# One fused layer on one Trainium2 core: the second gate, the residual and the last expert's factor moved

## What is computed

```python
xbc = silu(conv(xbc))                      # 4 taps along the tokens, 2560 channels
scores = einsum(C, B) * decay * dt         # inside chunks of 128 tokens
y = (scores @ X + (C * exp(cum)) @ Hprev + D_skip * X).reshape(B, L, D_INNER)
y = rmsnorm(y * silu(z), gnorm_w)          # "y * silu(z)" is the gate
x = x + layernorm(u + y @ out_proj_w.T)    # the residual
...
w = silu(einsum(h, down_embed[indices]) * softmax(top 8 of scores))
x = x + layernorm(silu(h @ W_up.T) @ W_down.T + einsum(w, up_embed[indices]))
```

## Time and profile before

| what | value |
|---|---|
| median of 3 runs (lowest to highest) | 2841.09 us (2840.73 to 2841.52) |
| the profiled execution, its own time | 2840.37 us |
| span of its trace, first to last instruction | 2838.7 us |
| mean granted TensorE clock | 0.972 |
| busy: PE, PEld, DVE, ACT, POOL | 95%, 78%, 86%, 61%, 74% |
| HBM read and written | 25.37 MB, 8.39 MB (12 GB/s) |

### The profile page before, as it was taken

The page is one execution under the profiler, slowest core; times in us unless marked ns, Lnnn a source line. Parts: engine busy times, 40 slices in busy tenths (PEclk is TensorE's granted clock), DMA queues, the critical chain, the costliest instruction groups (busy, mean ns, idle before and its releaser), DMA issues. The chain is left out here.

```text
span 2838.7 us, 50280 instructions
## 1 busy us (share of the span) xinstructions
PE 2684.0 (95%) x14720; PEld 2215.7 (78%) x14720; DVE 2449.3 (86%) x6310; ACT 1737.2 (61%) x3656; POOL 2100.9 (74%) x2689
## 2 busy tenths in 40 slices
PE   5899999999999999999999999999999999999985
PEld 4778887878887878887878887878887878887864
DVE  4588898998888998889898889988889988989985
ACT  4566666666666566666666666666666666666643
POOL 3377777877777877777877777877777877777866
PEclk9999999999999999999999999999999999999998
DMA  3000000000000000000000000000000000000000
GB/s 133 8 8 12 5 7 11 11 11 11 4 7 11 11 11 11 4 7 11 11 11 11 4 7 11 11 11 11 4 7 11 11 11 8 7 7 11 8 5 8
DMA packets 28182, 34.23 MB, mean 12 GB/s; under 512 B 2672, under 2 KB 27248, under 8 KB 27440
## 3 DMA queue, kind: packets, MB, share of 16 engines
q1 hardware_dynamic: 28144, 33.77, 3.8%
HBM read 25.37 MB, written 8.39 MB: 12 GB/s over the span
## 5 line engine op out<-in xcount | busy, mean ns | idle before, releaser
L1079 DVE SCALAR_TENSOR_TENSOR acc<-bank,cw,acc 128x253 f32<-128x253 f32 (+2 forms) x1920 | 773.5, 470 | 0.0
L1405 PE MATMUL bank<-hT,w_in 128*128 128x256 f32 x2560 | 606.3, 382 | 11.4 <-DVE acc L1079 10.8
L594 POOL TENSOR_TENSOR Em<-ee 128x1024 f32<-128x1024 f32 x256 | 578.8, 2280 | 11.3 <-issue 11.3
L1405 PEld LDWEIGHTS bank<-hT,w_in 128*128 128x128 f32 x2560 | 485.0, 192 | 118.2 <-issue 44.5
L1238 DVE SCALAR_TENSOR_TENSOR Em<-Em,p 128x1024 f32<-128x1024 f32 x256 | 407.1, 1590 | 0.0
L609 POOL TENSOR_TENSOR W<-W,Em 128x1024 f32<-128x1024 f32 x128 | 337.0, 2633 | 8.5 <-ACT Em L887 0.3
L755 ACT ACTIVATE acc<-bank,cb,cw 128x256 f32<-128x256 f32 x640 | 325.1, 561 | 0.0
L1247 DVE TENSOR_TENSOR Em<-Em,products 128x1024 f32<-128x1024 f32 x256 | 310.9, 1214 | 4.5
L887 ACT ACTIVATE Em<-Em,rden 128x1024 f32<-128x1024 f32 x256 | 292.0, 1142 | 33.9 <-DVE Em L1247 33.9
L1574 PE MATMUL products<-w_de,h2T 128*128 128x512 f32 x512 | 234.5, 601 | 17.7 <-DVE Em L1247 17.7
L736 ACT ACTIVATE xbcT<-acc 128x512 f32<-128x512 f32 x320 | 200.6, 627 | 74.1 <-DVE acc L1079 74.0
(11 more groups left out here) (196 smaller groups left out, 5578.9 us busy)
## 6 DMA issues: line engine op xcount, KB each, us to landing
x_in<-x_dram SPq DMA_DIRECT2D x32, 256.0 KB, 2.7
x_res<-x_dram SPq DMA_DIRECT2D x32, 256.0 KB, 2.7
out_dram<-f SPq DMA_DIRECT2D x32, 256.0 KB, 2.2
w_in<-in_wT_dram SPq DMA_DIRECT2D x1, 3080.0 KB, 12.0
w_up<-upT_dram SPq DMA_DIRECT2D x1, 1024.0 KB, 14.7
w_de<-down_eT_dram SPq DMA_DIRECT2D x1, 1024.0 KB, 16.7
w_down<-downT_dram SPq DMA_DIRECT2D x1, 1024.0 KB, 18.7
w_ue<-up_e_dram SPq DMA_DIRECT2D x1, 1024.0 KB, 20.8
```

Of the source, the lines that this page charges most:

```text
L594: nc.gpsimd.tensor_tensor(Em[:, k], bc(ee[:, k, 0:XD], 2, KEYS), bc(ee[:, k, XD:XD + KEYS], 1, XD), ALU.mult).then_inc(E_done.sem, 1)
L1079: ins = V.scalar_tensor_tensor(acc[:, r, a, ahead:], ps[:, a * TOK:(a + 1) * TOK - ahead], cw[:, t, k:k + 1], acc[:, r, a, ahead:], ALU.mu ...
L1405: last = mm(ring[j % 2][:, a * TOK:(a + 1) * TOK], w_in[:, k, at:at + P], hT[:, k, :], start=k == 0, stop=k == DK - 1)
```

## The change

- VectorE: `tail_residual(e)` comes ahead of convolution 0. `ffn_mask(e, 0, 2)` goes from before the second gate to behind the state step. `ffn_choose` multiplies all of `clz` by `rden` in one instruction (128x160); `ffn_last` is the copy of `last_a` alone.
- ScalarE: the silu of `clz` takes `last_a` as its scale; `ffn_norm(f)` goes behind the second square.
- GpSimd: the map of chunk 1, head 0 waits for the second gate. The order is then: root of y, map of head 1, `tail_root3(g)`, `tail_root4(g)` (before: in the next turn), first sum of `W`, maps of heads 2 and 3. The second decay of the state goes ahead of `ffn_root`.
- TensorE: no clearing matmul; the first product of `ffn_down` starts the bank.

```diff
 def weigh(e, c, *heads, gate=None):
+    if gate is not None:
+        pool.wait_ge(y_done.sem, y_done.at(gate, CH - 1))
...
 # GpSimd's do_group
-                if b:
-                    tail_root4(e)
...
                     mixer_scale(g, 1)
+                    mixer_decay(g, 1)
                 if c:
                     ffn_root(f)
-                if a:
-                    mixer_decay(g, 1)
-                if b:
-                    weigh(e, 1, 0, 1)
+                if b:
+                    weigh(e, 1, 0, gate=g)
                 if a:
                     mixer_root_y(g)
                 if b:
+                    weigh(e, 1, 1)
+                if a:
+                    tail_root3(g)
+                    tail_root4(g)
+                if b:
                     collect(e, 0, 1)
-                if a:
-                    tail_root3(g)
-                if b:
                     weigh(e, 1, 2, 3)
...
 # ScalarE, ffn_experts; ffn_norm(f) moves from behind mixer_yT(g, 0) to behind mixer_square(g, 1)
-                    nc.scalar.activation(cls[:], clz[:, c], ACT.Silu, accum_out=clsum[:, c:c + 1])\
+                    nc.scalar.activation(cls[:], clz[:, c], ACT.Silu, scale=last_a[:, 0:1],
+                                         accum_out=clsum[:, c:c + 1])\
...
 # VectorE
+                V.tensor_tensor(masked, masked, bc(rden[:].rearrange("p c h -> p (c h)"), 2, NC), ALU.mult)\
...
-                V.scalar_tensor_tensor(clz[:, c], clz[:, c], last_a[:, 0:1], bc(rden[:, c], 2, NC),
-                                       ALU.mult, ALU.mult).then_inc(clz_done.sem, 1)
...
-                conv(0)
                 if b:
                     tail_residual(e)
-                conv(1)
+                conv(0, 1)
...
                     ffn_times(e, 0, 1)
-                    ffn_mask(e, 0, 2)
                 if a:
                     mixer_gate(g, 1)
                     mixer_step(g, 1)
                 if b:
+                    ffn_mask(e, 0, 2)
                     ffn_times(e, 0, 2)
...
 # TensorE, ffn_down
-                    mm(f0[:], zero_b[:], mask_b[:].rearrange("p h t -> p (h t)"), start=True, stop=False)
...
-                              start=False, stop=False)
+                              start=c == 0 and i == 0, stop=False)
```

More of the change, by code:

```diff
@@ L123, in sandwich @@
         ident_b = sb("ident_b", [P, P], BF16)
-        zero_b = sb("zero_b", [P, P], BF16)
         mask_b = sb("mask_b", [P, 4, P], BF16)
@@ L270, in sandwich @@
         Z_done = sig("Z_done", CH * RH)
-        clz_done, cls_done = sig("clz_done", CH), sig("cls_done", CH)
+        clz_done, last_done, cls_done = sig("clz_done"), sig("last_done", CH), sig("cls_done", CH)
         W_part, W_done = sig("W_part", CH * (RH - 1)), sig("W_done", CH)
@@ L341, in _ @@
             nc.gpsimd.memset(mask_b[:], 0.0).then_inc(own_pool, own.one())
-            nc.gpsimd.memset(zero_b[:], 0.0).then_inc(own_pool, own.one())
             nc.gpsimd.memset(halo[:], 0.0).then_inc(own_pool, own.one())
@@ L582, in tail_root4, with weigh @@
                 nc.gpsimd.tensor_tensor(shift4[:], rs4[:], neg_mean4[:], ALU.mult).then_inc(root4.sem, 1)
-            def weigh(e, c, *heads):
+            def weigh(e, c, *heads, gate=None):
+                if gate is not None:
+                    pool.wait_ge(y_done.sem, y_done.at(gate, CH - 1))
                 for h in heads:
@@ L654, in do_group @@
                 if b:
-                    collect(e, 0, 1)
+                    weigh(e, 1, 1)
                 if a:
                     tail_root3(g)
+                    tail_root4(g)
                 if b:
+                    collect(e, 0, 1)
                     weigh(e, 1, 2, 3)
@@ L875, in ffn_experts @@
                 if 0 in heads:
-                    act.wait_ge(clz_done.sem, clz_done.at(e, c))
+                    act.wait_ge(clz_done.sem, clz_done.at(e))
+                    act.wait_ge(last_done.sem, last_done.at(e, c))
                     if c or later(e):
@@ L994, in do_group @@
                     mixer_yT(g, 0)
-                if c:
-                    ffn_norm(f)
                 if b:
@@ L1001, in do_group @@
                     mixer_square(g, 1)
+                if c:
+                    ffn_norm(f)
                 if b:
@@ L1221, in ffn_choose @@
                 V.reciprocal(rden[:].rearrange("p c h -> p (c h)"), den[:]).then_inc(rden_done.sem, 1)
+                dve.wait_ge(rden_done.sem, rden_done.at(e))
+                dve.wait_ge(own_dve, own.n)
+                V.tensor_tensor(masked, masked, bc(rden[:].rearrange("p c h -> p (c h)"), 2, NC), ALU.mult)\
+                    .then_inc(clz_done.sem, 1)
             def ffn_last(e, c):
                 dve.wait_ge(A_ps.sem, A_ps.at(e, c))
-                dve.wait_ge(rden_done.sem, rden_done.at(e))
-                V.tensor_copy(last_a[:], fA[:, EXPERTS - 1:]).then_inc(own_dve, own.one())
-                dve.wait_ge(own_dve, own.n)
-                V.scalar_tensor_tensor(clz[:, c], clz[:, c], last_a[:, 0:1], bc(rden[:, c], 2, NC),
-                                       ALU.mult, ALU.mult).then_inc(clz_done.sem, 1)
+                if c or later(e):
+                    dve.wait_ge(cls_done.sem, cls_done.at(e, c - 1))
+                V.tensor_copy(last_a[:], fA[:, EXPERTS - 1:]).then_inc(last_done.sem, 1)
             def ffn_mask(e, c, *heads):
```

## The result

The changed kernel takes 2936.55 us (median of 4 runs, 2934.81 to 2941.0) against 2841.31 us before: ratio 1.034, 95% interval 1.032 to 1.036, some 95 us slower. The forecast was 2903 us, slower, with a range up to 2958. The execution with the trace took 2941.0 us by itself, 4.5 above the median.

What follows compares the result with a forecast made beforehand. TensorE, busy 95%, was taken as the bound, waiting 2.13 us a turn for the second gate. A turn: +0.63 - 0.2 + 1.63 = +2.06 us; 30 turns give +62 on 2841.09, so 2903 us, range 2830 to 2958.

Steps and rivals of the forecast that it cites:

- The gate: TensorE's 2.13 us wait for the second gate, and the 1.63 us clock fall behind it, go each turn.
- What is late next: At mixer_pair 2, TensorE waits 4.4 us for convolution 0 and starts 0.63 us later than before.
- the one by the addition: On VectorE, GpSimd's map of head 1 asks 0.35 us earlier; the store's addition ends at 1373.75, not 1372.4.
- step 5: VectorE's mask and ffn_times of head 3 end at 1376.15; ffn_A also waits for this, about 0.2 us.
- 11.66: TensorE's microseconds at full clock from the transposes to pair 2, making it ready there at 1379.5.
- Step 7: VectorE's residual and convolution 0 take 4.51 us with GpSimd quiet, ending at 1383.9.
- The clock: TensorE's clock falls behind pair 2 as it fell behind the gate, costing 1.63 us more a turn.
- rival B: Stall moves to pair 2, clock stays low longer, losing 3.4 us: +3.85 a turn, 2956 us; chance 0.20.
- A: Stall moves to pair 2 with one clock fall of 1.63 us: 2903 us; chance 0.48.
- The clearing matmul: On TensorE, dropping this 0.38 us matmul saves between 0 and 0.38 us a turn; 0.2 taken.
- The factor: On VectorE, ffn_last loses a multiplication per chunk and ffn_choose gains one of 128x160; nothing taken.
- The rule weighed: By the skill's shared-port rule, ffn_root's power on GpSimd could delay the gate some 0.7 us; not counted.

Runs made afterwards that it cites:

- e7: Changed kernel with GpSimd's map of chunk 1, head 1 moved behind root 3 and root 4: 2874.9 us, ratio to before 1.012.
- e1: Changed kernel with convolution 0 ahead of the residual again on VectorE, all else as changed: 2918.1 us, ratio to before 1.027.
- e2: Changed kernel plus five unneeded matmuls on TensorE between ffn_A and pair 2, filling the wait: 2877.4 us, ratio to before 1.013.
- e3: Kernel before plus the residual part alone: residual ahead of convolution 0, root 4 right behind root 3: 2873.3 us, ratio 1.013.
- e6: Kernel before with two unneeded matmuls filling the gate's wait and without the clearing matmul: 2795.2 us, ratio 0.984.
- e11: Kernel before plus the last expert's factor part alone (one 128x160 multiplication, last_a as silu scale): 2843.0 us, ratio 1.001.
- e9: Changed kernel with convolution 0 first, ffn_best behind convolution 7, tail_sum and residual later, GpSimd's map explicitly waiting for ffn_times: 2762.8 us, ratio 0.973.

## Why the prediction was right, and where it was off

It laid the new order out on the old turn's times. The new trace, moved by 1414.72 - 1364.17 = 50.55 us so that the product `Yn` stands where it did, gives:

| step | forecast | measured |
|---|---|---|
| gate ends | 1367.5 | 1367.58 |
| mask of head 2 ends | 1370.55 | 1370.64 |
| store's addition ends | 1373.75 | 1373.90 |
| head 3 done, the sum begins | 1376.15 | 1376.27 |
| root 3 ends | 1379.3 | 1379.42 |
| convolution 0 ends | 1383.9 | 1384.37 |
| pair 2 waits | 4.4 | 4.32 |

1. **The gate.** Right: its wait of 2.13 went, and the clock's fall behind it too.
2. **What is late next.** Right in its place (pair 2 for convolution 0) and in each detour; e7 confirms the one by the addition; that convolution 0 stands behind the residual e1 confirms, where pair 2 waits 1.33 with the two exchanged. Small misses add up to 0.5: the residual begins 0.30 after the root's end (1429.97 to 1430.27), and residual and convolution take 4.65 instead of 4.51. Pair 2 begins 1384.42 - 1383.27 = 1.15 later than before, not 0.63. That the wait itself came out at 4.32 against 4.4 is partly luck: TensorE was ready at 1384.42 - 4.32 = 1380.10 and not at 1379.5, mostly because it had waited 0.40 at `ffn_A`, which step 5 named with 0.2 and left out of the 11.66. Both ends of the wait were some 0.5 late. (Step 7 also rounds up: 1379.3 + 4.51 is 1383.8.)
3. **The clock.** The mis-sized term. The fall was forecast to cost 1.63 as before, on the argument that one fall is like the other; it costs 2.37 (e2). The text had named the reason against itself, that the new wait of 4.4 is nearer to the one of 4.82 in the earlier trace rows, behind which the clock lost 3.4, and left that to rival B. B's 3.4 is 1.0 above what was measured, A's 1.63 is 0.7 below. B's total of 2956 us came out nearer, 20 us off against A's 34, but partly because the small misses of points 2 and 4 make up for over half of its overshoot. What decides how far the clock falls was not found: behind equal waits of 2.13 us e3 loses 1.4 to 3.0 and once nothing, and behind equal waits of 3.50 us e7 loses nothing 9 times in 28 and up to 2.9 otherwise.
4. **The clearing matmul.** 0.2 us a turn was taken, e6 shows 0.7 us in all. From pair 2 to the next turn's `Yn` (1503.46) it is 68.5 us, and before it was 66.2: +2.3, which is the clock's 2.4 with hardly anything off for the clearing.
5. **The factor.** Nothing was taken; e11 agrees within 2 us.

The sum: 1.15 + 2.27 = 3.42 us a turn instead of 2.06. Over 28 steady distances that is 96 of the 100.6 us between the two traced executions (2941.0 - 2840.37). The forecast's 62 was right in sign and mechanism and a third too small, half of the miss in point 3 and half in points 2 and 4.

**The rule weighed.** Whether small operands on GpSimd could hold up the gate was not put to the test: `ffn_root`'s power ended 0.4 us ahead of the gate's multiplication. The reading that the sum went by is borne out by e9, where a whole mask (1449.93 to 1451.21, its plain 1.28 us) runs inside a power of 128x16 (1449.13 to 1452.07). The other way round e1 shows a VectorE subtraction of only 128x64 elements that waits 1.8 us for GpSimd's 128x1024 sum. The Trainium skill, "SBUF — State Buffer", section "SBUF: two separate sides", has it that whichever starts first gets the shared ports for the whole instruction and the other fully blocks; for the large instructions of GpSimd this agrees, for the power of 128x16 it does not.

## What to carry to other kernels

When two engines hold each other up, moving one instruction out of the other's way moves everything behind it too: lay the new order out on the old times as far as the next wait of the engine that bounds the kernel, and beyond it to the end of the turn, since e1's new stall came 40 us later than the one it replaced. TensorE may lose the clock as well as the time when it waits, so price a stall as wait plus fall, and the fall as a range (here nothing to 3.0 us); filling the wait with matmuls that nobody needs took 44 us off the kernel before, with no other change. Place the short instructions on which a matmul waits by an explicit wait of the other engine, not by hoping that they ask first; e9 does so and its pair 2 no longer waits, though it moves other things as well.

## What had not been expected of the hardware

Behind waits of the same length the granted clock stayed low for different times: 0.50 over 3.42 us and 0.68 over the next 3.40 in one turn of e3, 0.55 over 3.39 and then 0.95 in another, both behind 2.12 to 2.13 us of idle time. Behind 9 of 28 waits of 3.50 us in e7 it did not fall at all. In the kernels before and after, the steady turns all had the same within 0.1 us. And two instructions of GpSimd in a row don't shut VectorE out for both: in e1 one subtraction got through between the sums (2.47 us for the two of line 1180), and only the one behind it, handed over after the second sum had begun, was held up again.
